# Two-layer model on one core: expert tiles fetched two steps ahead, layer 0's step reordered, layer 1's token logits by transposes

## The chip, the cores and the metric

One NeuronCore of one Trainium2 chip. The metric is device time in microseconds (us) of one execution of the whole program. All matrices are float32.

## The reference, cut to what matters

The input is 16 sequences of 256 tokens with 128 features. Four blocks follow each other, each with a residual and a layer norm behind it.

```python
x = ln(x + rwkv(x))        # L0 attention: time mixing, then channel mixing
x = ln(x + moe(x))         # L0 FFN: top-1 of 8 experts, 128 -> 1024 -> (512, gated) -> 128
x = ln(x + linear_att(x))  # L1 attention: relu(q), relu(k), 16 heads of 8
x = ln(x + soft_moe(x))    # L1 FFN

# time mixing: k, v, r = mixes of ln(x) and its predecessor, times Wk, Wv, Wr
#   per channel, over t: numerator and denominator decay, with a running peak for the exponentials
#   x += (sigmoid(r) * numerator / denominator) @ Wo
# channel mixing: x += sigmoid(xr @ Wr) * (square(relu(xk @ Wk)) @ Wv)

# soft_moe
logits   = xn @ slots.T                  # 256 tokens by 512 slots
dispatch = softmax(logits, over tokens)  # slots = dispatch.T @ xn
combine  = softmax(logits, over slots)   # out = combine @ (gelu(slots @ w1) @ w2)
```

## The kernel before, in words

Everything is written engine by engine, each engine's program in one order, with semaphores between them. The work is done for pairs of sequences (U = 2, called u = 0 and 1). There are three stages.

**Layer 0, time and channel mixing and routing** (about 0 to 237 us). `pipeline` (first one) runs a step for s = -2 to 8. In one step four parts of different turns are live: N (norm and transposition of turn s+2), M (time mixing of turn s+1), C (channel mixing of turn s), R (routing of turn s-1). The steps s = 2 to 5 are a hardware loop of full steps "NMCR", the others are written out with the parts that exist.

TensorE's order in a full step: k and v products (L606, L607) of both u; transposes of `normed2` (L601) of both u; the r products `tm_Wr`, into bank 0; transposes of `normed3` of both; channel keys 0 and 1 of both (cm_Wk); router logits (L685); for each u receptance (L625, L627) and keys 2 and 3; the output product of time mixing of u = 0 (L613); channel values (L703); transposes of `normed1`; ranks (L638, L642); output product of u = 1.

ScalarE's order: `h2_cols` of both u (L770); `normalise(3)` of u = 1 (L736); `shares(0)`, four relus (L745) and then three exponentials (L748, L750, L753) on which VectorE's recurrence of u = 0 waits; `xa_cols` (L779); `r_tanh` (L784); relus and squares of the channel keys with `shares(1)` between; `rc_tanh`; norm 1; `h1_cols`; norm 3 of u = 0; norm 2 of both.

VectorE: the running peak and `delta` of both u (L967, L971), statistics of the next input, the recurrence of u = 0 and 1 (`take` L977, scan L984, L992, L998, reciprocal L1002, `y_cols` L1011) with the routing choice between; then the residual sums, with statistics behind each: `second_sum(0)` (L1108, L1112), `first_sum(0)`, `first_sum(1)` (L1101), `second_sum(1)`. `stats` is two bn_stats (L958) and, after a wait for them, two bn_aggr (L961); one `moments` buffer serves all.

GpSimd turns variances into reciprocal deviations (L853 to L858), adds x and x1 (L913), computes places, and writes the rows of a turn to their sorted places in HBM by four indirect DMAs (`scatter`, L892). In step s = 7 (parts "CR") it scatters before it turns the variances of norm 3 around. SP copies `normed3` into `stage` (L572), after the scatter of the turn before has landed; the last step's VectorE waits for the same thing before it writes `slot_now`.

**Experts** (about 237 to 373 us). Tiles of 128 sorted rows, 39 used of 40, two per step (u = 0, 1), 20 steps. `expert_pipeline` has T (transpose of the fetched rows `xg`, L443) two steps ahead, F (w1 products, L436: four gate, four linear blocks) one ahead, S (w2 products, L426). TensorE's step: for each u S and F; then T of both u. There is one `xg` buffer for each u, so GpSimd fetches (L522) the rows of a tile only after the transposition of the tile before, and reads its row number from a table in between. SP loads w1 of each tile (512 KB, L399), the first four loads in a row. The loop has two steps in each iteration.

**Layer 1** (about 373 to 740 us). One sequence per step. `pipeline` (second one) has G, E (gather of expert rows, norm), A (attention), F (soft-MoE routing), B (slots' FFN and combination), C (final norm) live at once; the loop covers most of the 16 sequences. In F TensorE computes the logits twice: transposed, slots on partitions, into banks 2 and 3 (`by_slot`, L1396, 8 passes of 256 columns), and tokens on partitions, into banks 4 and 5 (by token, L1434, 4 passes of 512 columns). VectorE takes the peak of the first over the tokens in one reduction of 1024 elements (`slot_peak`, L1681), TensorE turns it (L1406), VectorE makes `slot_shift` (L1698), the by-token logits are reduced to `token_peak` (L1734), and TensorE adds the shifts into the banks (L1457, L1485) before the exponentials (L1545, L1553). TensorE's order around it: by-slot logits, hidden chunks 0 and 1 (L1362), turned peak, chunk 2, q transposes and k-v products, chunk 3, attention products (L1427), by-token logits (L1434), attention transposes (L1344), process chunk 0 (L1368), output product (L1448), process chunk 1, shift (L1457), process chunks 2 and 3. VectorE's order between the attention products and the shift: normaliser and `att` (L1717 to L1721), sum and statistics of the next sequence (L1727, L1646, L1649), `token_peak`.

A float32 matmul is two passes, shown as two MATMUL rows; a transpose is one.

```python
for u in range(U):                       # experts_gpsimd, in each step
    settle(pool, xg_turned[u], s + 3, pool_passed)
    row = pool.value_load(tile_rows[0:1, bass.ds((s + 2) * U + u, 1)], ...)
    pool.dma_start(xg[u][:, :], sorted_x[bass.ds(row, P), :]).then_inc(xg_loaded[u], 16)
```

## Time and profile before

| | |
|---|---|
| median of 3 runs | 739.71 us (737.86 to 739.84) |
| profiled execution | 742.24 us, span 740.5 us |
| TensorE | 655.2 us busy, 88% of the span |
| VectorE, ScalarE, GpSimd | 465.5, 368.6, 271.7 us busy (63, 50, 37%) |
| mean granted TensorE clock | 0.95 |

The span runs from the first to the last instruction; the execution's own time is 1.7 us longer. The time lost on TensorE is in the first two stages: by forty equal slices its busy tenths there vary from 4 to 9 while layer 1 holds 9 nearly throughout.

### The profile page before, as it was taken

How to read it: one execution, taken by the hardware profiler on the slowest of the kernel's cores; microseconds unless marked ns; L12 is line 12 of the kernel's file. 1: busy time of each engine (PE TensorE's matmuls, PEld its weight loads, DVE VectorE, ACT ScalarE, POOL GpSimd, SP SyncE). 2: the span in 40 equal slices, each digit the busy share in tenths (PEclk: the TensorE clock that was granted, in tenths of full speed). 3: DMA queues.
4: the chain of work that ended last, by engine and by line, in shares of the span. 5: the costliest groups of instructions: out<-in, count | busy, mean ns of one | idle time of the engine just before them, and what ended most of it. 6: DMA issues, size and time to landing. Idle time of an engine off the chain costs nothing. (4 is left out here: it accounts for less than half of the span.)

```text
span 740.5 us, 14606 instructions
## 1 busy us (share of the span) xinstructions
PE 655.2 (88%) x4043; PEld 524.0 (71%) x4044; DVE 465.5 (63%) x1390; ACT 368.6 (50%) x818; POOL 271.7 (37%) x574
## 2 busy tenths in 40 slices
PE   4499899999672798989978899999999999999995
PEld 3487788988561798888934577777776777777773
DVE  4888889887624243444425577776777776777632
ACT  4388777888531343444401445545554544445542
POOL 2323766586454111111134324444333433333200
PEclk9699999999785799999999999999999999999999
DMA  4071111111014565666400000000000000000000
GB/s 139 28 230 43 58 58 43 64 64 40 33 43 133 172 216 174 209 213 200 133 21 8 7 8 15 15 14 14 14 14 14 7 11 11 14 15 8 8 8 14
DMA packets 39457, 46.98 MB, mean 63 GB/s; under 512 B 5184, under 2 KB 31104, under 8 KB 39424
## 3 DMA queue, kind: packets, MB, share of 16 engines
q1 hardware_dynamic: 35520, 39.50, 17.1%
q0 software_dynamic: 3328, 6.82, 3.0%
q8 instruction: 15, 0.25, 0.1%
q10 hardware_dynamic: 576, 0.26, 0.1%
q14 instruction: 18, 0.15, 0.1%
HBM read 34.58 MB, written 7.80 MB: 57 GB/s over the span
## 5 line engine op out<-in xcount | busy, mean ns | idle before, releaser
L436 PE MATMUL banks<-xg_cols,w 128*128 128x128 f32 x624 | 79.5, 283 | 0.0
L463 ACT ACTIVATE gate<-banks,b_cols 128x128 f32<-128x128 f32 x156 | 44.5, 367 | 68.9 <-PE banks L436 68.9
L493 DVE SCALAR_TENSOR_TENSOR hidden<-banks,b_cols,gate 128x128 f32<-128x128 f32 x156 | 44.0, 345 | 55.3 <-ACT gate L463 52.4
L436 PEld LDWEIGHTS banks<-xg_cols,w 128*128 128x128 f32 x624 | 76.4, 200 | 0.0
L1368 PE MATMUL banks<-ffn_w,act_cols 128*128 128x128 f32 x512 | 66.2, 278 | 0.7 <-ACT act_cols L1514 0.7
L1368 PEld LDWEIGHTS banks<-ffn_w,act_cols 128*128 128x128 f32 x512 | 60.8, 192 | 8.4 <-issue 6.8
L1362 PE MATMUL banks<-slots_cols,ffn_w 128*128 128x512 f32 x128 | 64.1, 606 | 0.8 <-ACT slots_cols L1529 0.8
L522 POOL DMA_DIRECT2D xg<-sorted_x x40 | 21.8, 546 | 106.4 <-issue 95.5
L1514 ACT ACTIVATE act_cols<-banks 128x512 f32<-128x512 f32 x64 | 38.2, 597 | 28.2 <-PE banks L1362 28.2
L426 PE MATMUL banks<-w,hidden 128*128 x312 | 42.6, 280 | 8.8 <-issue 8.2
L426 PEld LDWEIGHTS banks<-w,hidden 128*128 128x128 f32 x312 | 38.3, 193 | 11.3 <-issue 11.3
L601 PE MATMUL banks<-consts,normed 128*128 128x128 f32 x96 | 19.7, 320 | 29.9 <-ACT normed L736 29.9
L1580 POOL TENSOR_TENSOR rstd_b<-mean_var_b,eps 128x2 f32<-128x2 f32 x16 | 3.1, 195 | 115.0 <-DVE mean_var_b L1649 115.0
L892 POOL DMA_INDIRECT sorted_x<-stage,slot_now x32 | 33.3, 1040 | 18.4 <-issue 13.3
L606 PE MATMUL banks<-h_cols,cm_Wk_now 128*128 128x256 f32 x128 | 39.6, 392 | 0.0
L607 PE MATMUL banks<-h_cols,cm_Wk_before 128*128 128x256 f32 x128 | 38.9, 386 | 0.0
L853 POOL TENSOR_TENSOR rstd<-mean_var,eps 128x2 f32<-128x2 f32 x48 | 10.3, 215 | 76.5 <-DVE mean_var L961 76.4
L856 POOL TENSOR_TENSOR rstd<-rstd,neg_half 128x2 f32<-128x2 f32 x48 | 36.8, 767 | 4.0
L601 PEld LDWEIGHTS banks<-consts,normed 128*128 128x128 f32 x96 | 12.8, 161 | 35.8 <-ACT normed L736 27.2
L1553 ACT ACTIVATE combine<-banks 128x1024 f32<-128x1024 f32 x16 | 16.4, 1023 | 39.2 <-PE banks L1485 39.2
L1569 POOL DMA_INDIRECT y_got<-sorted_y,y_idx x32 | 32.4, 1013 | 9.3 <-issue 7.5
L1492 PE MATMUL banks<-processed,combine 128*128 128x129 f32 x256 | 32.8, 281 | 0.8 <-DVE processed L1750 0.8
(240 smaller groups left out, 1630.1 us busy)
## 6 DMA issues: line engine op xcount, KB each, us to landing
w<-w_dram SPq DMA_DIRECT2D x39, 512.0 KB, 3.4
xg<-sorted_x POOLq DMA_DIRECT2D x40, 64.0 KB, 2.9
sorted_y<-y_rows SPq DMA_DIRECT2D x39, 64.0 KB, 2.3
x_in_rows<-x_dram SPq DMA_DIRECT2D x16, 128.0 KB, 2.2
x_res<-x_dram SPq DMA_DIRECT2D x16, 128.0 KB, 2.2
xa<-normed SPq DMA_DIRECT2D x16, 128.0 KB, 2.0
stage<-normed SPq DMA_DIRECT2D x16, 128.0 KB, 2.1
out_dram<-final SPq DMA_DIRECT2D x16, 128.0 KB, 1.8
```

The source lines that it names most:

```text
L426: last = pe.matmul(dst, hidden[u][:, c, :], w2[:, bass.ds(e2, 1), c, :].squeeze(1), start=(c == 0), stop=(c == XC - 1))
L436: last = pe.matmul(bank(u, k, c * P, (c + 1) * P), w1[parity][u][:, lo:lo + P], xg_cols[u][:, :], start=True, stop=True)
L463: act.activation(gate[u][:, c, :], bank(u, 2, c * P, (c + 1) * P), ACT.Sigmoid, bias=b1_cols[:, bass.ds(e1 * GC + XC + c, 1)]).then_inc(ga ...
L493: last = dve.scalar_tensor_tensor(hidden[u][:, c, :], bank(u, 1, c * P, (c + 1) * P), b1_cols[:, bass.ds(e1 * GC + c, 1)], gate[u][:, c, : ...
L606: pe.matmul(dst, now[:, lo:hi], h[:, 1:T + 1], start=True, stop=False)
L607: return pe.matmul(dst, before[:, lo:hi], h[:, 0:T], start=False, stop=True)
L856: p.step(pool.tensor_tensor(rstd[u][:, :], rstd[u][:, :], neg_half[:, 0:NT], ALU.pow))
L892: pool.indirect_dma_start(sorted_x, bass.IndirectOffsetOnAxis(ap=slot_now[:, t:t + 1], axis=0), stage[u][:, j, :], None).then_inc(scattere ...
L1362: pe.matmul(banks[:, 6 + c % 2, :], ffn_w1[:, c * P:(c + 1) * P], slots_cols[ub][:, :], start=True, stop=True).then_inc(S["hid_ready"][ub], 1)
L1368: last = pe.matmul(banks[:, 6, s * D:(s + 1) * D], act_cols[ub][:, c, s * P:(s + 1) * P], ffn_w2[:, c, :], start=(c == 0), stop=(c == HC - 1))
L1492: last = pe.matmul(banks[:, 7, j * N129:(j + 1) * N129], combine[ub][:, s, j * P:(j + 1) * P], processed[ub][:, s, :], start=(s == 0), sto ...
L1514: act.activation(act_cols[ub][:, c, :], banks[:, 6 + c % 2, :], ACT.Gelu).then_inc(S["gelu_ready"][ub], 1)
```

## The change

Experts: two `xg` buffers for each u (by step parity). GpSimd fetches four steps' worth ahead of S (two steps ahead of T) and reads row numbers before it waits. T of both u stands between u = 0 and u = 1 on TensorE. SP's first w1 loads of turn 1 wait for the first `xg` of both u. Layer 0: the r products go to bank 3, each in front of its u's `normed2` transposes; `r_tanh` goes in front of `shares(0)`; `normalise(3)` of u = 1 behind it; the fourth relu goes between the exponentials; `normed3`'s transposes alternate with the keys, u by u; VectorE's sums and statistics are interleaved, with a `moments` buffer for each norm; the scatter of step s = 7 moves to the end of GpSimd's step. Layer 1: by-token logits by eight transposes of a saved SBUF copy; VectorE makes that copy in four instructions that also give the peak; process chunk 0 goes in front of the attention transposes and chunk 1 in front of the output product.

```diff
@@ layer 0, buffers
-        moments = bufs("moments", [P, NT, 6])
+        moments = {k: bufs(f"moments_{k}", [P, NT, 6]) for k in (1, 2, 3)}
@@ experts
-        xg = bufs("xg", [P, D])
+        xg = [bufs(f"xg_{parity}", [P, D]) for parity in range(2)]
@@ experts_sync
             for turn in range(2):
+                if turn:
+                    for u in range(U):
+                        sp.wait_ge(xg_loaded[0][u], 16)
@@ experts_tensor, in the loop over u, behind F
-                for u in range(U):
-                    if "T" in parts:
-                        pe.wait_ge(xg_loaded[u], s * 16 + 48)
-                        pe.transpose(bank(u, 0, 0, P), xg[u][:, :], ident).then_inc(xg_turned[u], 1)
+                    if u == 0 and "T" in parts:
+                        for v in range(U):
+                            pe.wait_ge(xg_loaded[h][v], i * 16 + 32)
+                            if "F" in parts:
+                                pe.wait_ge(xg_cols_ready[v], s + 2)
+                            pe.transpose(bank(v, 0, 0, P), xg[h][v][:, :], ident).then_inc(xg_turned[v], 1)
@@ experts_scalar, now in the loop over u
                     if "T" in parts:
-                        act.wait_ge(xg_turned[u], s + 4)
+                        act.wait_ge(xg_turned[u], s + 3)
+                        if "F" in parts:
+                            act.wait_ge(lin_ready[u], s + 2)
@@ experts_gpsimd
+            def step(s, h):
+                for u in range(U):
+                    row = row_of(s + 4, u)
+                    settle(pool, xg_turned[u], s + 3, pool_passed)
+                    fetch(row, h, u)
             pool.wait_ge(tables_ready, 2)
+            first_rows = [row_of(0, u) for u in range(U)]
             pool.wait_ge(scattered, 16 * TILES)
             pool.wait_ge(zeroed_sem, 16 + 16 * E)
...
@@ layer 0, TensorE
+                    for u in range(U):
+                        if "M" in parts:
+                            if "C" in parts and follows(c):
+                                pe.wait_ge(R["rc_done"][u], c)
+                            mixed_columns(bank(u, 3, 0, T), h1_cols[u], "tm_Wr", 0, D
+                                          ).then_inc(R["r_ready"][u], 1)
+                        if "C" in parts:
                             pe.wait_ge(R["normed2_ready"][u], c * NT + NT)
                             turn(bank(u, 0), normed2[u], R["turned2"][u])
...
+                    for u in range(U):
+                        if "R" in parts:
                             pe.wait_ge(R["normed3_ready"][u], r * NT + NT)
                             turn(bank(u, 2), normed3[u], R["turned3"][u])
+                        if "C" in parts:
                             pe.wait_ge(R["h2_ready"][u], c + 1)
+                            if "M" in parts:
+                                pe.wait_ge(R["r_done"][u], m + 1)
                             for k in (0, 1):
                                 channel_keys(u, k, bank(u, 3, k * T, (k + 1) * T))
@@ layer 0, ScalarE: shares
+                        below(TAKE_OUT, -1.0, 0.0)
+                        below(TAKE_STATE, -1.0, U_PLUS_W)
+                        below(KEEP_STATE, 1.0, MINUS_U_W)
+                        act.wait_ge(R["args_ready"][u], m * 4 + 2)
                         act.activation(take[u][:, :, 1, :], below_peak[u][:, 0:2, :], ACT.Exp, scale=-1.0
                                        ).then_inc(R["exps_ready"][u], 1)
+                        below(KEEP_OUT, 1.0, 0.0)
...
+                    for u in range(U):
+                        if "C" in parts:
                             act.wait_ge(R["turned2"][u], c + 1)
                             act.activation(h2_cols[u][:, 1:T + 1], bank(u, 0, 0, T), ...)
+                        if "M" in parts:
+                            act.wait_ge(R["r_ready"][u], m + 1)
+                            act.activation(r_tanh[u][:, :], bank(u, 3, 0, T), ACT.Tanh, scale=0.5
+                                           ).then_inc(R["r_done"][u], 1)
                     if "M" in parts:
                         shares(0)
                     if "R" in parts:
+                        normalise(3, r, 1, gated, normed3)
                         for u in range(U):
                             act.wait_ge(R["turned3"][u], r + 1)
@@ layer 0, GpSimd
-                    if "R" in parts and "M" not in parts:
-                        if "C" in parts:
-                            find_places()
-                        scatter()
+                    if parts == "CR":
+                        find_places()
...
-                    if "R" in parts and "M" in parts:
-                        find_places()
+                    if "R" in parts:
+                        if "M" in parts:
+                            find_places()
                         scatter()
@@ layer 0, VectorE
                     if "C" in parts:
-                        second_sum(qc, c, 0)
+                        gate_values(qc, c, 0)
+                        gated0 = second_sum(qc, c, 0)
                     if "M" in parts:
+                        first_sum(qm, m, 0)
+                    if "C" in parts:
+                        spread(qc, 3, 0, gated0)
+                    if "M" in parts:
+                        dve.wait_ge(R["x1_ready"][0], m + 1)
+                        summed0 = stats(qm, 2, x1, 0)
+                        first_sum(qm, m, 1)
+                        if "R" in parts:
+                            places(r)
+                        spread(qm, 2, 0, summed0)
+                        dve.wait_ge(R["x1_ready"][1], m + 1)
+                        summed1 = stats(qm, 2, x1, 1)
+                    if "C" in parts:
+                        gate_values(qc, c, 1)
+                    if "M" in parts:
+                        spread(qm, 2, 1, summed1)
                         qm.close()
                     if "C" in parts:
-                        second_sum(qc, c, 1)
+                        gated1 = second_sum(qc, c, 1)
+                        spread(qc, 3, 1, gated1)
                         qc.close()
@@ layer 1, TensorE
+                            if s % 2:
+                                last.then_inc(S["by_slot_ready"][uf], 1)
...
+                        pe.wait_ge(S["slot_logits_ready"][uf], nf * SC + SC)
                         for j in range(NT):
-                            last = pe.matmul(banks[:, 4 + j, :], xn_cols[uf][:, j * P:(j + 1) * P], slot_cols[:, :],
-                                             start=True, stop=False, skip_group_check=True)
+                            for s in range(SC):
+                                last = pe.matmul(banks[:, 4 + j, s * P:(s + 1) * P],
+                                                 slot_logits[uf][:, s, j * P:(j + 1) * P], ident,
+                                                 is_transpose=True, start=(s == 0), stop=False,
+                                                 skip_group_check=True)
                         last.then_inc(S["by_token_ready"][uf], 1)
+                    if b:
+                        pe.wait_ge(S["gelu_ready"][ub], nb * HC + HC)
+                        process((0,))
...
@@ layer 1, VectorE
-                        dve.wait_ge(S["by_slot_ready"][uf], nf + 1)
-                        dve.tensor_reduce(slot_peak[uf][:, :], LT.rearrange("p b (c t) -> p (b c) t", t=T),
-                                          AX, ALU.max, negate=True).then_inc(S["slot_peak_ready"][uf], 1)
+                        for s in range(SC):
+                            dve.wait_ge(S["by_slot_ready"][uf], nf * 2 + s // 2 + 1)
+                            dve.tensor_scalar(slot_logits[uf][:, s, :], by_slot(s), 1.0, -3e38, ALU.mult, ALU.max,
+                                              accum_out=slot_top[uf][:, s:s + 1]).then_inc(S["slot_logits_ready"][uf], 1)
+                        dve.wait_ge(S["slot_logits_ready"][uf], nf * SC + SC)
+                        dve.tensor_scalar(slot_peak[uf][:, :], slot_top[uf][:, :], -1.0, None, ALU.mult
+                                          ).then_inc(S["slot_peak_ready"][uf], 1)
```

## Rows read from the trace of the kernel before

**Rows 1.** Timeline, VectorE, layer 0 (start us, busy us, engine, line, names [idle before]).

```profile
18.37 0.66 DVE L977 TENSOR_TENSOR take<-take,banks 128x512 f32<-128x512 f32 x1
...
62.45 0.69 DVE L977 TENSOR_TENSOR take<-take,banks 128x512 f32<-128x512 f32 x1 [1.35 <-ACT take L748]
...
180.02 0.69 DVE L977 TENSOR_TENSOR take<-take,banks 128x512 f32<-128x512 f32 x1 [2.82 <-ACT take L748]
...
217.23 0.25 DVE L961 BATCH_NORM_AGGREGATE mean_var<-moments 128x2 f32<-128x6 f32 x2 [0.15 <-DVE moments L958]
```

**Rows 2.** Timeline, TensorE, layer 0.

```profile
16.79 0.59 PE L607 MATMUL banks<-h_cols,tm_Wr_before 128*128 128x256 f32 x2
...
108.68 0.60 PE L606 MATMUL banks<-h_cols,cm_Wk_now 128*128 128x256 f32 x2
...
112.14 0.95 PE L685 MATMUL banks<-router_w,xa_cols 128*128 128x8 f32 x8
...
126.57 0.59 PE L607 MATMUL banks<-h_cols,tm_Wv_before 128*128 128x256 f32 x2
...
129.12 0.44 PE L601 MATMUL banks<-consts,normed 128*128 128x128 f32 x2 [1.21 <-ACT normed L736]
```

**Rows 3.** Timeline, ScalarE, layer 0.

```profile
130.06 0.86 ACT L736 ACTIVATE normed<-gated,shift,rstd 128x128 f32<-128x128 f32 x2
130.83 0.40 ACT L745 ACTIVATE below_peak<-delta 128x256 f32<-128x256 f32 x1
...
133.73 0.64 ACT L779 ACTIVATE xa_cols<-banks 128x256 f32<-128x256 f32 x2
```

**Rows 4.** Busy time by stretch, layer 0 (PE, PEld, DVE, ACT, POOL, clock, DMA, GB/s).

```profile
130.00:132.00 2.00, 2.00 (x8) 1.65 (x7) 1.66 (x10) 2.00 (x7) 1.76 (x6) 0.63 0.18 54
132.00:134.00 2.00, 2.00 (x9) 1.62 (x8) 0.95 (x4) 1.97 (x7) 0.90 (x3) 0.51 0.65 208
```

**Rows 5.** Timeline, TensorE, experts.

```profile
245.27 6.00 PE L436 MATMUL banks<-xg_cols,w 128*128 128x128 f32 x32
...
290.67 3.35 PE L436 MATMUL banks<-xg_cols,w 128*128 128x128 f32 x16
```

**Rows 6.** Waits, 237 to 376 us (total us, times, longest us).

```profile
PE banks L443 <- DMA xg<-sorted_x: 15.9, 5, 13.4
```

**Rows 7.** Timeline, GpSimd, end of layer 0 and start of the experts.

```profile
221.32 0.21 POOL L853 TENSOR_TENSOR rstd<-mean_var,eps 128x2 f32<-128x2 f32 x1
...
230.89 1.08 POOL L892 DMA_INDIRECT sorted_x<-stage,slot_now  x1 [5.19 <-DVE slot_now L1066]
...
238.67 0.59 POOL L522 DMA_DIRECT2D xg<-sorted_x  x1 [2.90 <-issue]
```

**Rows 8.** The page's part 6, DMA issues (count, KB each, us to landing).

```profile
xg<-sorted_x POOLq DMA_DIRECT2D x40, 64.0 KB, 2.9
```

**Rows 9.** Chain of waits, a looped step of layer 1 (start us, us).

```profile
504.30 0.44 PE banks L1388 x4
...
511.40 1.72 PE banks L1434 x4
```

**Rows 10.** Timeline, TensorE, the same step.

```profile
511.24 1.88 PE L1434 MATMUL banks<-slot_cols,xn_cols 128*128 128x512 f32 x4
...
515.50 0.60 PE L1457 MATMUL banks<-slot_shift,ones_bf 4*128 4x512 bf16 x2
```

**Rows 11.** Timeline, VectorE, the same step.

```profile
506.50 1.22 DVE L1681 TENSOR_REDUCE slot_peak<-banks 128x4 bf16<-128x1024 f32 x1 [0.85 <-PE banks L1396]
...
512.05 0.42 DVE L1721 TENSOR_TENSOR att<-banks,norm_inv 128x256 f32<-128x256 f32 x1
512.39 0.41 DVE L1727 TENSOR_TENSOR summed_e<-xa,y_got 128x256 f32<-128x256 f32 x1
...
513.65 1.19 DVE L1734 TENSOR_REDUCE token_peak<-banks 128x2 bf16<-128x1024 f32 x1
```

**Rows 12.** Groups of instructions by line (busy us, mean ns of one, idle us).

```profile
L814 ACT ACTIVATION_READ_ACCUMULATOR square_junk<-slot_rows 128x1 f32 x4 | 0.8, 192 | 0.0
```

98 lines of the change are left out of this document (37 added, 61 removed).

## The prediction

> **What bounds the kernel now.** I read the page's slices first: TensorE is at nine tenths in layer 1 and uneven before it. So each stage has its own limit, and I took each from its timeline, with the chain of waits and the waits for the causes. I sum against the profiled execution (742.24 us) and carry the difference to its median, 2.5 us lower.
>
> Layer 0 is bounded by a cycle, not by an engine. VectorE's recurrence of u = 0 starts at L977, and in each full step it stands waiting for ScalarE's exponential. Its start recurs five times between 62.45 and 180.02, every 23.5 us [rows 1]. TensorE is close behind: from the channel keys at 108.68 to the end of the last k and v product, 126.57 + 0.43 = 127.00, it works without a gap, 18.3 us [rows 2]. With the pieces in front (r products, transposes) it has some 20.9 us of work and idles some 2 us, 1.21 of it in front of the second `normed2` transposes. In two of those five steps the granted clock then falls: 0.63 and 0.51 over two stretches of 2 us, that is the lower level of 1.2 GHz for most of both, and work worth 0.37 x 2 + 0.49 x 2 = 1.7 us is lost [rows 4].
>
> The experts are bounded by TensorE with holes. It waits for the first `xg` until 243.7, 13.4 us by the waits, and starts F at 245.27; four later waits for `xg` make 2.5 us together [rows 5, 6]. In front of them are GpSimd's serial steps: scatter, landing, row number, fetch [rows 7].
>
> Layer 1 is bounded by TensorE's own work: the chain there is TensorE almost alone, and the by-token logits stand in it with 1.72 us in each looped step [rows 9].
>
> **Layer 0, part by part.** (a) First step with M: `shares(0)` now stands behind both `r_tanh`, so behind the last r product, which ends issuing at 16.79 + 0.43 = 17.2 [rows 2]. With the semaphore (0.2) and one tanh (0.3) the relus start at 17.7; three relus (1.1) and the exponential (0.65) end at 19.5, where VectorE started at 18.37 [rows 1]: +1.2. (b) In step s = 0 ScalarE needs, ahead of `shares(0)`, an r product (0.87), a transposition of 0.2, its own two h columns and two tanh; against before 1.9 more, less 0.45 for the fourth relu moved and its wait gone: +1.4. (c) Then the cycle from the sums onward is shorter by the relu and by a tanh traded against `normalise(3)`: -0.5.
>
> (d) Full steps. `normed3` of u = 1 now comes after `shares(0)`, and TensorE's in-order queue has its transposes between the keys of u = 0 and u = 1. Everything behind them waits: half the keys, logits, receptance, channel values, the next k and v. This makes a new cycle. TensorE from these transposes to the second `normed2` transposes: 18.3 less the keys of u = 0, half of 112.14 - 108.68 = 3.46 [rows 2], makes 16.6; plus the transposes themselves 0.2, the two r products 1.7 (eight passes of 256 columns, like half the keys) and the first `normed2` transposes 0.2: 18.7. ScalarE from there: 0.5 until the transposes are readable, h columns 0.45, tanh 0.3, `shares(0)` 133.73 - 130.83 = 2.9 less 0.1 of wait, `normalise(3)` 0.86 and a semaphore 0.05 [rows 3]: 5.0. Sum 23.7, against 23.5 on average before: +1.0 over five steps. TensorE's idle time, about 2.8 us, now lies in one piece. Before, idling of about 2 us in two pieces was followed by a fall of the clock in two of five steps; now each fall is paid in full, because TensorE is in the cycle. I take 2.5 falls at 1.7 us: +4.2; bounds none and six (+10). (e) The last M step: channel values end 0.8 later: +0.8. (f) Step s = 7: keys of u = 0 no longer wait for `normed3` of u = 1, at the lower clock: -1.5. VectorE's interleaved sums save about 1 us a step (waits of 0.15 [rows 1]), but GpSimd, four deviations of 1.4 us in a row, does not deliver earlier: nothing; if GpSimd were faster it would be worth up to the 1 us. Together +6.6, bounds -2.5 and +13.
>
> (g) The scatter. In s = 7 the statistics are ready at 217.5 but GpSimd turns to them at 221.32, behind four scatters [rows 1, 7]: the logits behind them come 3.8 us earlier. But the scatter now follows, from about 222.9 to 229.1 landed, and three things are queued behind that: SP's two `stage` copies, VectorE's `slot_now`, and GpSimd itself. `slot_now` gains 0.6, the stage copies (about 2.2 us after 229.1) lose: the last scatter starts near 232.1 instead of 230.89 [rows 7], +1.2.
>
> **Experts.** Start: the fetch comes 1.2 later by (g) and 0.8 earlier as the row number is already read: about 239.0 against 238.67 [rows 7]. It then landed only at 243.7, 5 us, beside four w1 loads; with two of them held back I take the median landing of 2.9 [rows 8], nearest to a fetch among one or two loads. The second is 0.6 later, transposes, copy: F at 242.5 instead of 245.27, -2.8 (bounds 0 and -4). The held loads are wanted only at the second F, about 249. Loop: the fetch has a whole step, 5.6 us, more. The in-loop waits are 2.5 less 0.86 at the start = 1.6 [rows 6], their restarts about 0.3 each; after one of them the clock fell, sixteen passes took 3.35 where they take 1.95: 1.4 [rows 5]. -4.0 (bounds -2 and -5). `xg_cols` of u = 1 now waits for F of u = 1, which is hidden by the next step's S and F of u = 0 (2.7 us); without them it would cost 0.6 a step. The loop's own gap of about 1 us in every second step stays. Together -6.8.
>
> **Layer 1.** Four transposes take 0.44 [rows 9], eight 0.87, against 1.72: -0.85 on TensorE. Before, the shift (L1457) started at 515.50, 4.26 after the by-token logits' start at 511.24 [rows 10]. Now TensorE would be there after 3.4, at 514.65. But the shift needs VectorE's `token_peak`, which follows `att` and the statistics and ends at 513.65 + 1.19 = 514.84 whatever TensorE does [rows 11]; with the semaphore 514.94. So only 0.56 comes through. The two process chunks moved forward fill the ScalarE latencies; cover gone, they'd cost up to 0.4.
>
> The peak: 256 elements are 0.34 from start to start (512.05 to 512.39). VectorE idles 0.85 before the old reduction at 506.50, and the first two copies go there. End with the negation: 505.75 + 4 x (0.34 + x) + 0.25, x the cost of the accumulator's output; the old reduction let the next go at 507.64. The slip for q and k rows, on which TensorE stands, is near 4x - 0.28. No row shows an accumulating VectorE instruction. Below, x = 0; above, ScalarE's own accumulator read, 0.19 [rows 12]. That row is the nearest; less the 0.08 by which VectorE's neighbours overlap (0.42 busy, 0.34 apart) it gives x = 0.11, slip 0.16. Per step -0.40, 14 steps -5.6, the edge steps -0.9: -6.5 (bounds -9.5 and -1).
>
> The row shows a separate read on ScalarE. The Trainium skill, "VectorE: DVE Perf Modes", section "Two Vector instructions with no wait between them", says that a VectorE op which writes out its accumulator is two instructions. By it x is above 0 and layer 1 gains 6.5 rather than 9.5; no run here shows it yet.
>
> **Sum:** +6.6 - 6.8 - 6.5 = -6.7, so 735.5 profiled and 733.0 as a median.
>
> **Rivals.** (B) Layer 0 does not lose. If `normed3` of u = 1 is there in time, or ScalarE's earlier exponential (0.5 a step) decides, layer 0 gives -2.5, the sum is -15.8, 724. For: ScalarE is named in each wait of L977. Against: TensorE's 18.7 us leave no room. (C) The clock falls after every idle piece: six falls instead of 2.5 put 6 us on, 739. (E) The change does not do what it says for the experts: `xg` is late because the w1 loads fill the queues, not because it is issued late. Then about 6.8 is missing: 739.8. Against: waits come only with late issues. (D) Slower: the accumulating copies. From x = 0.25 the slip passes 0.8 a step and layer 1 turns from gain to loss by enough to outweigh the rest; at x = 0.3 the slip is 0.92 to 1.0, +0.4 a step, +5 in layer 1, +4.8 in all, 744.5. Against: that is above ScalarE's 0.19.
>
> **Numbers.** Forecast 0.43 (own range 729 to 738), B 0.23, C 0.13, E 0.09, D 0.12. Range 722 to 742: from B to C and E, leaving out most of D. A measurement of this kernel tells 0.3%, 2.2 us, from no change. Faster: most of the forecast, B, a little of C and E: 0.71. Same: 0.15. Slower: D and the worst of C: 0.14.
>
> **What would show it.** Layer 0: TensorE waiting some 2.8 us for ScalarE's L736 between two pairs of keys; L977 at 23.7 us or more. Experts: F some 3 us earlier, no wait of L443 for DMA in the loop. Layer 1: step near 19.8 instead of 20.2, L1457 released by `token_peak`, the copies 0.34 to 0.53 apart. Wrong if layer 0 as a whole is shorter, or if a copy costs over 0.55.

## Result and profile of the changed kernel

The changed kernel takes 715.69 us (median of 4 runs, 714.66 to 716.76), the kernel before 739.13 us (4 runs, 737.86 to 739.84): a ratio of 0.9685, 95% interval 0.9663 to 0.9706, so 23.4 us or 3.2% faster. Forecast were 733.0 us and a range of 722 to 742: the direction was right, the gain was more than three times the forecast, and the range did not hold it.

The page's head and its line for TensorE:

```profile
span 713.0 us, 14924 instructions
...
PE 633.4 (89%) x4107; PEld 522.3 (73%) x4108; DVE 470.3 (66%) x1518; ACT 366.8 (51%) x818; POOL 272.0 (38%) x574
```

The profiled execution took 714.66 us against 742.24: 27.6 us less. Four marks cut this pair into stages: the start of the last scatter, the first F product, the last S product, the end of the span.

| stretch | before | after | difference | forecast |
|---|---|---|---|---|
| start to last scatter | 234.81 | 237.66 | +2.85 | +7.8 |
| last scatter to first F | 10.46 | 7.30 | -3.16 | -4.0 |
| first F to last S | 125.74 | 110.20 | -15.54 | -4.0 |
| last S to the end | 369.5 | 357.8 | -11.65 | -6.5 |

Experts: the timeline of TensorE, after, answers to [rows 5]. Its columns are start, busy us, engine, line, and in brackets idle time in front and its releaser. The second fence is the view of waits of TensorE in the experts' loop (total us, times, longest us), the third the same view of before.

```profile
244.96 3.69 PE L439 MATMUL banks<-xg_cols,w 128*128 128x128 f32 x16
...
355.16 1.15 PE L429 MATMUL banks<-w,hidden 128*128 x8 [0.52 <-DVE hidden L497]
```

```profile
PE banks L429 <- DVE hidden L497: 0.5, 1, 0.5
```

```profile
PE banks L426 <- issue: 8.2, 10, 1.2
PE banks L443 <- DMA xg<-sorted_x: 1.7, 3, 0.9
```

F starts only 0.3 us earlier, but all the rest of the stage is gapless: not one wait for `xg`, and not one of the ten holes of 8.2 us in front of the S products, which the prediction took for the loop's own. Every looped step is now 5.58 us from T to T; before, counted from the T at 251.11, ten of the eighteen distances from one T to the next were longer, by 0.24 to 4.14 us, 14.5 together.

Layer 0, VectorE's and TensorE's timelines, after, and TensorE's waits from 60 to 200 us; they answer to [rows 1, 2]:

```profile
62.55 0.69 DVE L997 TENSOR_TENSOR take<-take,banks 128x512 f32<-128x512 f32 x1 [1.96 <-ACT take L765]
...
86.08 0.69 DVE L997 TENSOR_TENSOR take<-take,banks 128x512 f32<-128x512 f32 x1 [1.84 <-ACT take L765]
...
111.27 0.69 DVE L997 TENSOR_TENSOR take<-take,banks 128x512 f32<-128x512 f32 x1 [1.56 <-ACT take L765]
...
181.85 0.69 DVE L997 TENSOR_TENSOR take<-take,banks 128x512 f32<-128x512 f32 x1 [3.10 <-ACT take L765]
```

```profile
88.00 0.69 PE L617 MATMUL banks<-consts,normed 128*128 128x128 f32 x2 [2.50 <-ACT normed L750]
88.48 1.06 PE L622 MATMUL banks<-h_cols,cm_Wk_now 128*128 128x256 f32 x2
...
113.20 0.44 PE L617 MATMUL banks<-consts,normed 128*128 128x128 f32 x2 [2.50 <-ACT normed L750]
113.47 0.60 PE L622 MATMUL banks<-h_cols,cm_Wk_now 128*128 128x256 f32 x2
```

```profile
PE banks L617 <- ACT normed L750: 14.7, 6, 2.5
```

The new wait is where it was forecast, between the two pairs of keys, released by ScalarE's `normed`: 2.50 us of idle time at 88.00 and at 113.20. The period is 23.53 us where the clock holds. Once it doesn't: behind the wait at 88.00 a pair of key passes takes 1.06 us, behind that at 113.20 it takes 0.60, and this one period is 25.19.

GpSimd at the end of layer 0, after, answers to [rows 7]: the last four scatters wait for the `stage` copy, as worked out in term (g), and the first fetch comes 2.5 us later than before.

```profile
233.87 0.95 POOL L910 DMA_INDIRECT sorted_x<-stage,slot_now  x1 [4.08 <-DMA stage<-normed]
...
237.66 0.96 POOL L910 DMA_INDIRECT sorted_x<-stage,slot_now  x1 [0.30 <-issue]
241.16 1.17 POOL L523 DMA_DIRECT2D xg<-sorted_x  x2 [2.54 <-DMA sorted_x<-stage,slot_now]
```

Layer 1. The first fence is TensorE and VectorE around the by-token logits of a looped step, after ([rows 10, 11]); the second gives the groups of the copies (busy us, mean ns of one, idle us):

```profile
509.90 1.04 PE L1476 MATMUL banks<-consts,slot_logits 128*128 128x128 f32 x8
510.77 1.06 PE L1407 MATMUL banks<-ffn_w,act_cols 128*128 128x128 f32 x8
...
513.54 0.60 PE L1501 MATMUL banks<-slot_shift,ones_bf 4*128 4x512 bf16 x2 [0.16 <-DVE token_peak L1782]
...
504.64 0.08 DVE L1726 DVE_READ_ACCUMULATOR slot_logits<-banks 128x1 f32 x1
504.64 0.42 DVE L1726 TENSOR_SCALAR_CACHE_REDUCE slot_logits<-banks 128x256 f32<-128x256 f32 x1
...
504.99 0.42 DVE L1726 TENSOR_SCALAR_CACHE_REDUCE slot_logits<-banks 128x256 f32<-128x256 f32 x1
...
512.29 1.19 DVE L1782 TENSOR_REDUCE token_peak<-banks 128x2 bf16<-128x1024 f32 x1
```

```profile
L1726 DVE TENSOR_SCALAR_CACHE_REDUCE slot_logits<-banks 128x256 f32<-128x256 f32 x64 | 24.1, 420 | 0.8
...
L1726 DVE DVE_READ_ACCUMULATOR slot_logits<-banks 128x1 f32 x64 | 5.3, 83 | 0.0
```

The eight transposes start at 509.90 and give way after 0.87 us; the shift at 513.54 is released by `token_peak`. A copy is two records, 420 ns of work and 83 ns of accumulator read, yet one copy starts 0.35 us after the other: the read costs 0.01 us, not the 0.11 of the prediction. The Trainium skill, "VectorE: DVE Perf Modes", section "Two Vector instructions with no wait between them", says that such an op is two instructions; the two groups agree, with 64 records each. From the fourth projection of queries, keys and values to the last, looped steps take 19.70 us on average (422.37 to 658.78) instead of 20.24 (442.11 to 684.95), 0.54 less. The shift starts 3.64 us behind the by-token logits instead of 4.26.

The edge of layer 1 holds something that is not the change's. The first projection of queries, keys and values, and the busy times of the stretch in which the granted clock (the third number from the end) was low there; two fences of before, then two of after:

```profile
383.42 2.93 PE L1382 MATMUL banks<-w_qkv,cols 128*128 128x384 f32 x4 [0.56 <-ACT cols L1550]
```

```profile
382.00:386.00 4.00, 3.01 (x6) 1.72 (x7) 0.44 (x3) 0.38 (x1) 1.95 (x2) 0.64 0.12 33
```

```profile
367.57 1.56 PE L1421 MATMUL banks<-w_qkv,cols 128*128 128x384 f32 x4 [0.56 <-ACT cols L1594]
```

```profile
358.00:362.00 4.00, 4.00 (x7) 1.53 (x6) 0.24 (x2) 0.00 (x0) 2.00 (x2) 0.61 0.06 16
```

Before, the granted clock was 0.64 from 382 to 386 us, at these four products; after, it was 0.61 from 358 to 362 us, at filler products that nothing waits for.

### The profile page after: what moved, and what is told of

Read it like the earlier page. It is cut to its first block, busy times and chain, and to the rows that moved or that the text cites. A ratio compares the mean times of both kernels' runs of the same rounds, so it can differ in the third digit from the quotient of the medians.

```text
span 713.0 us, 14924 instructions
## 1 busy us (share of the span) xinstructions
PE 633.4 (89%) x4107; PEld 522.3 (73%) x4108; DVE 470.3 (66%) x1518; ACT 366.8 (51%) x818; POOL 272.0 (38%) x574
## 4 chain that ended last, share of the span: by engine, by line
PE 38%; DVE 8%; issue 2%; POOL 1%; ACT 1%; DMA 0%; DVEq 0%; POOLq 0%; ACTq 0%
PE banks L1401 8%; PE banks L1407 5%; PE banks L1523 5%; PE banks L1536 4%; PE banks L1435 4%; PE banks L1421 3%; DVE token_peak L1782 2%; PE banks L1383 2%; PE banks L1467 1%; PE banks L1501 1%; PE banks L1529 1%; PE banks L1457 1%; DVE moments_e L1690 1%; PE banks L1427 1%; DVE summed_e L1775 1%
## 5 line engine op out<-in xcount | busy, mean ns | idle before, releaser
L439 PE MATMUL banks<-xg_cols,w 128*128 128x128 f32 x624 | 77.8, 279 | 0.0
L439 PEld LDWEIGHTS banks<-xg_cols,w 128*128 128x128 f32 x624 | 74.4, 196 | 0.2 <-issue 0.2
L622 PE MATMUL banks<-h_cols,cm_Wk_now 128*128 128x256 f32 x128 | 41.1, 405 | 0.2 <-ACT r_tanh L794 0.2
L1523 PE MATMUL banks<-xn,dispatch 128*128 128x129 f32 x256 | 34.2, 288 | 0.2 <-ACT dispatch L1589 0.2
```

Of the source, the lines that this page charges most:

```text
L439: last = pe.matmul(bank(u, k, c * P, (c + 1) * P), w1[parity][u][:, lo:lo + P], xg_cols[u][:, :], start=True, stop=True)
L622: pe.matmul(dst, now[:, lo:hi], h[:, 1:T + 1], start=True, stop=False)
L1523: last = pe.matmul(dst, dispatch[uf][:, j, s * P:(s + 1) * P], xn[uf][:, j, :], start=(j == 0), stop=(j == NT - 1))
```

## Experiments

Each kernel was timed beside the kernel before; ratios are to it. Runs 1 to 4, 5 to 8, 9 to 12, and 13 with 14 each shared a chip.

**1. Experts' part alone.** Edit: the four experts' functions and their buffers as in the diff; layers 0 and 1 as before.

> The kernel before with the experts' part of the change alone. Additive theory: the two traces put the last expert product's start 15.9 us earlier after the change (371.01 to 355.16), of which layer 0 and the scatter cost about 2.5, so the experts by themselves gave 15.5 in the loop and 2.8 at the first F, 18 in that one pair of executions; the profiled execution of before was some 2.5 us longer than its median, so by medians 14 to 18: 721 to 725 us, every looped step 5.58 us, no idle time of the S products other than for VectorE's hidden. Rival, that the experts' gain needs the other parts (the later end of layer 0 or layer 1's order): under 10 us, 730 or more. Prediction on record: 6.8 us, 732.

719.61 us (719.37 to 721.07), ratio 0.9764, interval 0.972 to 0.9808; 17 us by the medians of its batch (736.61). First F to last S takes 110.30 us, as in the changed kernel; from the last scatter to the first F it takes 8.05 us, 2.4 less than before. The experts' part needs no help, and it is most of the gain.

**2. Two buffers, T at the end of the step.**

```diff
-                    if u == 0 and "T" in parts:
-                        for v in range(U):
-                            pe.wait_ge(xg_loaded[h][v], i * 16 + 32)
...
+                for u in range(U):
+                    if "T" in parts:
+                        pe.wait_ge(xg_loaded[h][u], i * 16 + 32)
+                        pe.transpose(bank(u, 0, 0, P), xg[h][u][:, :], ident).then_inc(xg_turned[u], 1)
```

> The kernel before with the experts' two xg buffers, the early fetches, and the held w1 loads, but with both transposes T still at the end of the step, behind F of u = 1, and ScalarE's copies behind both. It tells the two theories of the loop's holes apart. Run-ahead theory: the about 1 us in front of every second S is TensorE's sequencer, held by the wait for an xg that lands just when T is due, so that the expert's number and the loop's end are read only after it; with xg there two steps ahead the holes go though T stands last: steps of 5.58 to 5.65 us, the time within 2 us of the experts-only kernel. Loop-end theory: the hole is the loop's end, bare because only two short transposes stand in front of it; it stays, 0.5 to 1.2 us in each second step, 6 us or more in all, so the time is 6 us or more above the experts-only kernel, and only the waits for DMA go.

720.82 us (718.96 to 721.39), ratio 0.9774, interval 0.9727 to 0.982; 110.45 us from first F to last S. The view of waits of its whole stage shows the one for the very first `xg` and a short one at the last S:

```profile
PE banks L446 <- DMA xg<-sorted_x: 11.1, 1, 11.1
PE banks L429 <- DVE hidden L494: 0.5, 1, 0.5
```

T stands last, right in front of the loop's end, as before, and the holes are gone. The loop-end theory falls for a kernel whose `xg` is there in time: the place of T is then worth nothing (0.15 us), the earlier fetch everything.

**3. One buffer, T in the middle.** Edit: T and its copies placed as in the change, `xg` single, fetched as before.

> The kernel before with T of both u moved between u = 0 and u = 1 on TensorE (and ScalarE's copies with it), but one xg buffer for each u, fetched one step ahead as before; no early row numbers, no held w1 loads. Loop-end theory: sixteen products of F stand in front of the loop's end now, the regular holes go (about 6 us), and only the late landings stay (8 us in the trace of before, with their restarts): 733, steps mostly 5.6 with three or four of 7 and more. Run-ahead theory alone: an xg that is late is as late in the middle, TensorE waits there for the same landings, and the time stays within 3 us of before, though the holes may move from S to T.

733.78 us (731.71 to 740.36), ratio 0.9966, interval 0.9932 to 1.0; 120.34 us from first F to last S, with late landings in the loop of 0.33 and 0.37 us where before had 0.87, 0.54 and 0.26. That is 5.4 less than the 125.74 of before, but only 2.4 less than the same experts take in kernel 4 (122.78), and 2.8 us by the medians.

```profile
264.40 0.38 PE L445 MATMUL banks<-consts,xg 128*128 128x128 f32 x2
265.17 1.15 PE L426 MATMUL banks<-w,hidden 128*128 x8 [0.39 <-issue]
...
276.26 0.38 PE L445 MATMUL banks<-consts,xg 128*128 128x128 f32 x2
277.16 1.15 PE L426 MATMUL banks<-w,hidden 128*128 x8 [0.51 <-issue]
...
288.19 0.72 PE L445 MATMUL banks<-consts,xg 128*128 128x128 f32 x2
289.55 1.15 PE L426 MATMUL banks<-w,hidden 128*128 x8 [0.63 <-issue]
```

```profile
PE banks L445 <- DMA xg<-sorted_x: 15.0, 4, 13.6
PE banks L426 <- issue: 5.2, 10, 0.7
```

The holes moved with T: they now stand in front of the S product of u = 1, in the middle of the step, far from the loop's end. So a hole belongs to the S behind T, wherever T is. The loop's end is not wholly without part in it: of the ten holes of before, the eight at a loop's end are 0.31 to 1.23 us long, the two elsewhere 0.39 and 0.26, and in the middle of the step all ten are 0.34 to 0.65.

**4. Layer 1's part alone.**

> The kernel before with layer 1's part alone (by-token logits by transposes of the copy, the four copies with peaks, the process chunks moved); four semaphores of the experts get the other scope, which moves no instruction. The traces of before and after differ by 11.65 us from the last expert product to the end: 14 looped steps at 0.46 make 6.4, the rest is at the edges, and 1.4 of that is the projection of the first step, which ran at a granted clock of 0.64 before and at 1.00 after. If the edge's clock hangs on layer 1's own order, this kernel gains 10 to 12 (728); if it is the luck of what came before it, 7 to 10 (731). Prediction on record: 6.5 (733).

726.12 us (724.97 to 731.39), ratio 0.9876, interval 0.9816 to 0.9936: 10.5 us. From last S to the end 356.95 us; no projection is long. Its experts are those of before, again with ten holes in front of S (8.17 us), yet first F to last S takes 122.78 us and not 125.74: it had two late landings in the loop (0.65 and 0.41 us) for three, and no F of 3.35 us. So the 15.5 us of the pair of traces is the upper end of what the experts' loop gives; against this execution it is 12.6.

**5. The expert's number read ahead of T.** On the kernel of experiment 3:

```diff
+                early = expert_of(s, 1) if "S" in parts and "T" in parts else None
                 for u in range(U):
                     if "S" in parts and u < pairs_of(parts, "S"):
-                        e2 = expert_of(s, u)
+                        e2 = early if u == 1 and early is not None else expert_of(s, u)
```

> The kernel of the one-buffer run with T in the middle (733.78 us, its holes now in front of the S product of u = 1, 0.34 to 0.65 us in ten steps, 5.2 us together), with one more edit: TensorE reads the expert number of that S at the start of the step, before T's wait, instead of behind it. Run-ahead theory in its narrow form: the hole is the reading of the number (a value load) that TensorE's sequencer can begin only when the late wait is over; read ahead of the wait it costs nothing, the holes of S go to under 0.1 us, and the time falls by up to 5 us (729 to 732), or by less if xg, asked for earlier relative to its use no more, is then waited for at T instead. Rival: whatever follows a late wait starts late, number or not (the semaphore's round trip, the queue run empty); the holes stay at 0.4 us or more and the time stays at 733 to 734.

731.4 us (729.12 to 737.49), ratio 0.9953, interval 0.9926 to 0.998; 118.39 us from first F to last S.

```profile
PE banks L446 <- DMA xg<-sorted_x: 16.3, 4, 13.4
...
PE banks L427 <- DVE hidden L497: 0.5, 1, 0.5
```

Behind T, where the holes were (5.2 us), none is left in this view. The run-ahead theory holds in its narrow form for them: the hole is the reading of a number from memory, which TensorE's sequencer begins only when the wait for `xg` is over. The Trainium skill, "Perfetto Trace Analysis", section "Sequencer Loop", has the sequencer push engine instructions into a queue but execute control instructions itself. That the hole goes with the reading agrees; that the wait keeps the sequencer from it is inferred.

A part of the holes has moved, though. In front of the first S behind each of the eight loop ends TensorE's weight loads idle 0.24 to 0.33 us, "issue", 2.3 us together (264.65 the first, 347.38 the last, timeline of weight loads). In this kernel two numbers are read there, right behind the loop's end; which of the two it is was not separated. And only 2 of the 5 us come back, by the stage's length. By the time not even that is shown: 0.9953 and 0.9966 lie within each other's intervals. Of the 8.1 us that this stage is longer than 110.30, 2.0 are waits for `xg` in the loop (1.19 and 0.80) and 2.3 the idling behind the loop's end; the rest was not traced. All of it goes with `xg` two steps ahead.

**6. Layer 0 as before** (the changed kernel without its layer 0 part).

> The changed kernel with layer 0 as before: experts' and layer 1's parts alone. If the parts add, the two single parts' ratios give 0.9764 x 0.9876 = 0.964, 3 us under the changed kernel (0.9685), and layer 0's part is a loss of about 3 us, of which the two traces show 1.8 in the cycle and 1.2 at the scatter. By the terms of the prediction (layer 0 +6.6, scatter +1.2) it would be 7.8 us faster than the changed kernel, 0.958. Rival, layer 0 gains or is even: 0.968 or above.

712.19 us (709.73 to 713.48), ratio 0.9687, interval 0.9653 to 0.9721. Taken by itself the ratio is the rival's (0.968 or above), the same as the changed kernel's 0.9685. But the kernel before took 734.51 us in this batch and 739.13 beside the changed one, so ratios of different batches don't order two kernels this close. Kernel 8, on the same chip, is the changed one but for the scatter and takes 716.89 us, 4.7 more. In the two profiled executions, 6.1 us apart, 2.7 stand at the last scatter (237.33 against 234.65) and 3.6 behind the experts, where kernel 8 has two long projections (see 9). In the pair of before and after the same marks give 1.8 us up to the eighth start of the recurrence and 1.0 from there to the last scatter. So layer 0's part is a loss of about 3 us.

**7. Shares and VectorE alone.** On kernel 6, the fourth relu between the exponentials and VectorE's interleaved sums:

```diff
-                        act.wait_ge(R["args_ready"][u], m * 4 + 4)
+                        act.wait_ge(R["args_ready"][u], m * 4 + 2)
                         act.activation(take[u][:, :, 1, :], below_peak[u][:, 0:2, :], ACT.Exp, scale=-1.0
                                        ).then_inc(R["exps_ready"][u], 1)
+                        below(KEEP_OUT, 1.0, 0.0)
```

> The kernel of the run with layer 0 as before, plus two pieces of layer 0's part: the fourth relu between the exponentials in shares, and VectorE's interleaved sums and statistics. TensorE's order, the place of the r products and of r_tanh, normalise(3) and the scatter stay as before. Theory: VectorE's start of the recurrence of u = 0 waits for ScalarE's exponential in every full step, and the relu (0.40 us) and its waits stood in front of it, so the period falls from 23.5 to 23.0 or 23.1; with the first steps 3 to 4 us off, ratio 0.959 to 0.961. Rival: TensorE's order is the bound (the exponential comes earlier, but the wait moves to the k and v products or to the transposes), and nothing is gained: equal to the run with layer 0 as before within 1 us.

708.66 us (707.38 to 710.63), ratio 0.9643, interval 0.961 to 0.9676; 3.5 us under kernel 6. The recurrence starts at 60.70 and, five periods on, at 175.86: 23.03 us a period, where before has 23.51 [rows 1]. As expected.

**8. Scatter in its old place.**

```diff
-                    if parts == "CR":
-                        find_places()
+                    if "R" in parts and "M" not in parts:
+                        if "C" in parts:
+                            find_places()
+                        scatter()
```

> The changed kernel with GpSimd's scatter of the last steps back in its old place (in front of the third norm's deviations in s = 7). Prediction's term (g): the moved scatter makes the last one start 1.2 us later, so this kernel is about 1.2 us faster than the changed one (ratio 0.967), its last scatter starting 1.2 us earlier relative to the recurrence. Rival: without the move the third norm's deviations wait behind four scatters again (3.8 us), the logits and the places of the last step come later, and this kernel is slower than the changed one by 0 to 2.6 us.

716.89 us (715.26 to 718.04), ratio 0.9747, interval 0.9715 to 0.9779. From the recurrence's eighth start to the last scatter 55.35 us, against 55.81 in the changed kernel. So the move costs 0.5 us, not 1.2, which the time can't show.

**9. The changed kernel again.**

> The changed kernel unaltered, as the measure for the runs beside it: 714 to 717 us. Its layer 1 is looked at for the granted clock of the first three query, key and value projections: in the profiled execution of before they ran at 2.93, 1.46 and 2.02 us, in the first one of the changed kernel at 1.56, 1.46 and 1.46. If that was the change's doing, the short ones come again; if it is the luck of where the clock falls while TensorE waits at the edge, one of the three may be long here.

716.87 us (716.28 to 718.46), ratio 0.9703, interval 0.967 to 0.9736. The timeline of TensorE at the start of layer 1:

```profile
368.08 2.92 PE L1421 MATMUL banks<-w_qkv,cols 128*128 128x384 f32 x4 [0.56 <-ACT cols L1594]
...
386.18 1.46 PE L1421 MATMUL banks<-w_qkv,cols 128*128 128x384 f32 x4
```

The first projection takes 2.92 us and the third, at 404.51, 1.92, in the same kernel that had 1.56 and 1.46 before. It is not the change's doing. From last S to the end: 361.2 us here, 357.8 there, so the two falls of the clock cost 3.4 us.

**10. Process chunks in their old places.** On kernel 7, `process((0,))` back behind the attention transposes and `process((1,))` behind the output product.

> The kernel of the run with shares and VectorE only (708.66 us), with layer 1's process chunk 0 back behind the attention transposes and chunk 1 back behind the output product; the by-token transposes and the copies stay. Theory: the moved chunks carry part of layer 1's gain (-0.5 to -0.6 us a step where TensorE's own saving is 0.85 less the wait for token_peak), because without a chunk in front of the attention transposes TensorE stands waiting for att, the reads of which end some 0.3 us after the by-token transposes: 0.2 to 0.4 us a step slower, 711 to 714. Rival, as the prediction had it: the gain is the transposes' alone and the chunks' place is worth nothing or costs cover behind the shift: within 1 us.

712.04 us (711.03 to 714.54), ratio 0.9637, interval 0.9604 to 0.9671. By the ratios it equals kernel 7 (0.9643); by the medians it is 3.4 us slower, and the medians are the better measure here, as the changed kernel on this chip and kernel 8, the same but for the scatter, on the other both take 716.9. The groups of TensorE from 415 to 640 us have a new idle time, in front of the attention transposes:

```profile
L1388 PE MATMUL banks<-consts,att 128*128 128x128 f32 x22 | 4.8, 300 | 2.9 <-DVE att L1774 2.9
```

2.9 us over eleven steps, 0.26 each; from last S to the end 363.2 us against 359.2 in kernel 7, both with a long third projection. By the traces the chunks' new places are worth 4 us: nearly half of layer 1's gain needs them as cover for the `att` on VectorE, which the shorter by-token logits would have laid bare.

**11. `token_peak` first.** On kernel 7:

```diff
+                    if f:
+                        dve.wait_ge(S["by_token_ready"][uf], nf * 2 + uf + 1)
+                        dve.tensor_reduce(token_peak[uf][:, :], L, AX, ALU.max, negate=True
+                                          ).then_inc(S["token_peak_ready"][uf], 1)
                     if e:
                         dve.wait_ge(S["y_gathered"][ue], ne * 16 * NT + 16 * NT)
```

> The kernel of the run with shares and VectorE only (708.66 us), with VectorE's token_peak reduction moved ahead of the sum and the statistics of the experts' residual (summed_e), which stand between att and token_peak for 1.2 us. Theory: in each looped step TensorE's shift product is released by token_peak, 0.16 us after the product in front of it; with the reduction 1.2 us earlier that wait goes in 14 steps, 2 to 3 us: 706. If the wait only passes to what is queued behind (xb 0.3 us later for the experts' deviations on GpSimd, then TensorE's xb transposes 2 us later), nothing is lost; rival: it is, and the time stays at 708.7 or rises by the 1.2 us of the reduction in front of the statistics in the first steps, where they are on the path: 708 to 711.

707.85 us (706.11 to 709.07), ratio 0.9583, interval 0.9549 to 0.9617: the fastest kernel here, 9 us or 1.3% under the changed kernel on the same chip (experiment 9). In the groups of TensorE the shift waits for nothing any more (first kernel 7, then this one):

```profile
L1506 PE MATMUL banks<-slot_shift,ones_bf 4*128 4x512 bf16 x22 | 6.6, 379 | 1.9 <-DVE token_peak L1787 1.9
```

```profile
L1506 PE MATMUL banks<-slot_shift,ones_bf 4*128 4x512 bf16 x22 | 6.6, 379 | 0.0
```

Its twelve steps from the projection at 416.82 to that at 651.36 average 19.55 us, the twelve of kernel 7 from 417.00 to 653.46 19.71. Its second step is 1.15 us longer (377.71 to 397.39, against 377.47 to 396.00), as the rival said of the first steps. So 0.16 us a step is gained and 1 us given back; the medians differ by 0.8 us, less than the spread of either kernel.

**12. The w1 loads not held.**

```diff
-                if turn:
-                    for u in range(U):
-                        sp.wait_ge(xg_loaded[0][u], 16)
```

> The kernel of the run with shares and VectorE only (708.66 us), without SP's wait for the first two xg in front of the second pair of w1 loads. Prediction's term: beside four w1 loads the first xg lands after 5 us instead of 2.9, so F starts 2 us later and so does the end: 710.7. Rival (E of the prediction, in small): the first xg is as fast without the hold, or F then waits less for its second pair of weights: within 0.7 us of 708.7.

712.71 us (710.75 to 713.59), ratio 0.9644, interval 0.961 to 0.9679. From the last scatter (230.97) to the first F (240.21) 9.24 us; the changed kernel (twice) and kernels 1, 2, 6 to 8, 10, 11, 13 and 14, which hold the loads, have 7.30 to 8.28. The hold is worth 1.0 to 1.9 us of the 3.2. The ratio is that of kernel 7 (0.9643), the median 4 us higher: the time does not settle it.

**13. `normalise(3)` in front of `shares(0)`.** On the changed kernel:

```diff
+                    if "R" in parts:
+                        normalise(3, r, 1, gated, normed3)
                     if "M" in parts:
                         shares(0)
                     if "R" in parts:
-                        normalise(3, r, 1, gated, normed3)
```

> The changed kernel with ScalarE's normalise(3) of u = 1 back in front of shares(0); everything else of layer 0's part, TensorE's order and r_tanh ahead of shares included, stays. The prediction's new cycle runs from the transposes of normed3 of u = 1 through TensorE's 18.7 us to ScalarE's h columns, tanh, shares(0), normalise(3) (5.0 us) and back. With normalise(3) ahead of shares(0) the 2.8 us of shares leave that cycle, TensorE no longer waits between the two pairs of keys, but the exponential comes 0.9 us later. If that cycle is the bound, the period falls below 23.5 (to about 23.0 to 23.3, set by the exponential again) and layer 0 ends 1 to 3 us earlier: 714. Rival: the bound is the recurrence's own path through r products, transposes, tanh and the exponential (the place of r_tanh and of the r products), and the 0.9 us come on top: period 24.0 to 24.4, 4 to 6 us slower: 721.

712.82 us (711.29 to 713.84), ratio 0.9665, interval 0.9625 to 0.9706. VectorE's recurrence and TensorE's waits from 60 to 200 us:

```profile
63.53 0.69 DVE L998 TENSOR_TENSOR take<-take,banks 128x512 f32<-128x512 f32 x1 [2.72 <-ACT take L765]
...
155.93 0.69 DVE L998 TENSOR_TENSOR take<-take,banks 128x512 f32<-128x512 f32 x1 [2.30 <-ACT take L765]
```

```profile
PE banks L617 <- ACT normed L750: 5.9, 3, 4.8
PE banks L699 <- ACT xa_cols L803: 3.0, 6, 0.5
```

The period is 23.07 us on average (63.53 to 178.87) and TensorE waits for `normed` 5.9 us in this stretch, where the changed kernel waits 14.7. The cycle through `normalise(3)` was the bound, as the prediction had it, and one line's place undoes it. The last scatter starts at 233.42, 4.2 us earlier than in the changed kernel and 1.4 earlier than before. (The medians come from different chips, and their ratios' intervals overlap.)

**14. Shares alone.** On kernel 6, the edit shown under 7 without VectorE's part.

> The kernel of the run with layer 0 as before (712.19 us), plus the fourth relu between the exponentials in shares, and nothing else of layer 0's part. The kernel that also had VectorE's interleaved sums took 708.66 us and its period was 23.03 us on average between the third and the eighth start of the recurrence, against 23.51. If the relu carries it, this one is the same as that within 0.7 us: 708 to 709.5. Rival: VectorE's interleaving carries it (GpSimd gets the moments earlier, so normed2 and the k and v products are earlier): the period stays at 23.4 to 23.5 and the time at 711.5 to 712.5.

709.14 us (708.5 to 711.59), ratio 0.9621, interval 0.9579 to 0.9662; period 23.12 us (61.84 to 177.42). The relu, with the shorter wait in front of the exponential, carries the gain of experiment 7; VectorE's interleaving adds about 0.1 us a step.

## Why the prediction was wrong in size

**The step that failed: "The loop's own gap of about 1 us in every second step stays."** It went, and with it most of the miss. The prediction counted in the experts' loop 1.6 us of waits, 0.9 of restarts and 1.4 of clock, 3.9 and rounded up to 4.0, and put every idle time named "issue" down to the loop. Experiment 2 shows that the loop's end costs nothing with T in front of it once `xg` is there in time, 3 that the holes follow T, and 5 that most of each is the number's reading behind a wait that ends late. A second thing was in view: each of the three late `xg` also had such a hole behind it (1.17, 1.13 and 1.23 us), and the first a slow F (3.35 us for 1.95); those three steps cost 8.2 us, the seven others 6.2. Term and measurement: -4.0 and -15.5, or -12.6 against the experts of kernel 4. Why nearly every second step has a hole and the others none was not traced. Two rows of before should have warned (timeline of TensorE):

```profile
257.45 1.15 PE L426 MATMUL banks<-w,hidden 128*128 x8 [0.39 <-issue]
...
263.61 1.15 PE L426 MATMUL banks<-w,hidden 128*128 x8 [0.31 <-issue]
```

The holes stand in front of two steps in a row, but a loop turn of two steps ends in front of only one of them.

**Layer 0: the mechanism right, the size too large.** TensorE's wait for ScalarE's `normed` (L736, now L750) was forecast at 2.8 us and is 2.50; the period was forecast at 23.7 and is 23.53. Experiment 13 shows the cycle. Too large were the falls of the clock (2.5 times 1.7 us; one, of 1.66, was paid) and the first steps (+2.1 by terms (a) to (c); by the third start of the recurrence 62.55 against 62.45). Terms (e) and (f) promised -0.7 behind the eighth start; kernel 8, which has them without the moved scatter, takes 0.6 us more than before from there to the last scatter (55.35 against 54.79), and that was not followed up. Rival B, that ScalarE's earlier exponential decides, gave the right value for the piece (0.4 us a step, experiments 7 and 14), but only where TensorE's order is left as it was. Term (g) was right in mechanism, the wait on `stage`, with 0.5 us for 1.2.

**Start of the experts.** -4.0 behind the last scatter forecast, -3.16 measured; TensorE has the first `xg` 2.8 us after its fetch instead of 5.0, as argued (experiment 12: 5.3 without the hold). The fetch itself comes only 0.4 us closer to the scatter where 0.8 was forecast, and F starts 1.0 us behind T where 0.6 was.

**Layer 1.** The forecast was -0.40 us a step, with x = 0.11 for the accumulator's read; x is 0.01 and the step -0.54, which is what the prediction's own sum gives at its lower end for x (-0.56, `token_peak` releasing the shift). So x is the mis-sized term. The chunks' places as cover, forecast at "up to 0.4", measured 0.26 us a step (experiment 10). Where no projection is long, last S to the end is 366.2 us with the old layer 1 (experiment 1) and 357.8 and 357.1 with the new (changed kernel, experiment 6): -8.4 to -9.1. The thirteen steps between the third projection and the last make -7.1 to -7.7 of it, the edges -1.3 to -1.4, for a forecast of -0.9. The other 3.3 of the 11.65 us in the pair of traces are the clock's, and they don't belong to the change (experiment 9).

**Rivals C, D, E.** C: six falls did not come. D: the accumulating copy costs 0.01 us where D needs 0.25. (By the prediction's own formula its slip at 0.25 is 0.72 us, not 0.8; that changes nothing here.) E: no `xg` waits though w1 loads land later than before (4.5 us in the median, 3.4 before), so the late issue was the cause.

By the marks: +2.85 - 3.16 - 15.5 - 8.4 = -24.2 us; the medians give -23.4.

## What to carry to other kernels

Idle time marked "issue" is not the loop's until the work in front of it has been looked at: where it follows a wait that ends just in time, a number read behind that wait is exposed, and an earlier transfer removes both; the cheap test is to move the wait and see whether the hole moves along. After such an edit look at the weight loads too: the row of the products can show no idle time where theirs still does (experiment 5). Price a hole by the distance of equal instructions in a step with it and a step without it, not by the idle column. And where two traces are compared, mark products that ran at the lower clock first: here 3 us of the difference between them were such a fall's.

## What the runs showed of the hardware

- Where TensorE reads a number behind a wait that ends late, 0.34 to 0.65 us of idle time stand there in the middle of a step (experiment 3), and 0.26 to 1.23 where the loop's end can fall in the same place (before). Read ahead of the wait it leaves none there, but 0.24 to 0.33 us of idle weight loads behind each loop end (experiment 5).
- VectorE's read of the accumulator is a record of 83 ns that adds 0.01 us between two copies of 420 ns.
- Where the granted clock falls at the start of layer 1 differs between two executions of one and the same kernel: on filler in the first profiled one of the changed kernel (sixteen passes in 8.80 us; 7.11 in the other), on the first and the third projection in experiment 9. That is worth 3.4 us.
